# Attention values weighted token by token: probabilities stationary, nine value columns moving

## The reference

```python
qkv = layernorm(x) @ Wqkv                                  # q, k rotated
allowed = (dist <= 0) & (dist >= -63)                      # a window of 64 keys
weights = softmax(where(allowed, q @ k.T / sqrt(8), -inf))
x = x + (weights @ v) @ Wout
xf = layernorm(x)
routed = sum over 4 chosen experts of gate * (silu(xf @ wg) * (xf @ wu)) @ wd     # capacity 640 a expert
x = x + shared(xf) + routed
```

## Time and profile before

| what | before |
|---|---|
| median of 3 runs | 617.76 us (612.9 to 621.51) |
| profiled execution, its time | 617.19 us |
| its span | 615.1 us |
| PE busy | 515.4 us (84%) |
| PE weight loads busy | 423.6 us (69%) |
| DVE, ACT, POOL busy | 419.5, 323.7, 354.9 us |
| L939 matmuls, 2048 records | 41.5 us busy |
| L1010 transposes, 128 | 17.7 us busy |
| L667 copies, 32 | 18.7 us busy |
| mean granted clock of TensorE | 0.942 |

### The profile page before, as it was taken

How to read it: one execution, slowest core, us unless ns; L and a number is a source line. 1 busy time by engine, 2 the same in 40 slices (tenths; PEclk the granted TensorE clock), 3 DMA queues, 4 the chain that set the end, 5 groups by cost and what they waited for, 6 DMA issues and landing times.

```text
span 615.1 us, 20844 instructions
## 1 busy us (share of the span) xinstructions
PE 515.4 (84%) x7427; PEld 423.6 (69%) x7427; DVE 419.5 (68%) x1281; ACT 323.7 (53%) x832; POOL 354.9 (58%) x394
## 2 busy tenths in 40 slices
PE   3669888988788888887556889999999998999855
PEld 2446666656565666666424569999999998999544
DVE  5677579968888899968553566666666666565255
ACT  3336676756766776656534325454555544554300
POOL 7510114456666666667766704777777776777700
PEclk9959888988999999979977899999999998999988
DMA  7898998976776775530000023544345454442099
GB/s 249 244 243 231 243 244 235 275 202 196 221 202 201 206 219 148 139 85 24 21 10 9 10 86 112 167 125 131 118 141 163 153 163 138 140 116 89 14 349 334
DMA packets 79418, 98.33 MB, mean 160 GB/s; under 512 B 12098, under 2 KB 60000, under 8 KB 79217
## 3 DMA queue, kind: packets, MB, share of 16 engines
q1 hardware_dynamic: 65280, 82.92, 46.4%
q0 software_dynamic: 9216, 12.02, 6.3%
q10 hardware_dynamic: 4848, 2.40, 1.3%
HBM read 50.00 MB, written 54.30 MB: 170 GB/s over the span
## 4 chain that ended last, share of the span: by engine, by line
PE 51%; SPq 11%; POOL 10%; DMA 9%; issue 8%; DVE 5%; ACT 5%; POOLq 1%; DVEq 0%; ACTq 0%
PE banks L1122 18%; PE banks L1148 11%; SPq L352 5%; POOL expert_slots L491 4%; DMA rotated_keys<-parts 4%; DMA rload<-pair_results 3%; PE banks L1133 3%; POOL pout L544 3%; SPq L393 2%; PE banks L967 2%; PE banks L957 2%; PE banks L939 2%; SPq L344 2%; PE banks L862 2%; PE banks L849 2%
## 5 line engine op out<-in xcount | busy, mean ns | idle before, releaser
L625 POOL DMA_INDIRECT pair_results<-yout,yidx x160 | 158.5, 990 | 69.7 <-issue 40.9
L491 POOL DMA_INDIRECT expert_slots<-xfe,sidx x128 | 128.1, 1000 | 89.7 <-issue 43.6
L1122 PE MATMUL banks<-xgT_parts,wgu_parts 128*128 128x320 f32 x768 | 131.7, 320 | 2.2 <-DVE hact L1508 1.9
L1122 PEld LDWEIGHTS banks<-xgT_parts,wgu_parts 128*128 128x128 f32 x768 | 114.1, 190 | 5.0 <-DVE hact L1508 2.5
L1246 DVE TENSOR_REDUCE mx<-banks 128x8 f32<-128x1024 f32 x64 | 78.1, 1220 | 24.9 <-PE banks L889 24.9
L662 ACT ACTIVATE pt<-banks 128x512 f32<-128x512 f32 x128 | 69.4, 594 | 46.2 <-PE banks L920 45.6
L1508 DVE TENSOR_TENSOR hact<-hact,banks 128x320 f32<-128x320 f32 x128 | 56.6, 482 | 45.7 <-ACT hact L793 43.9
L812 ACT ACTIVATE yout<-banks,ypair 128x128 f32<-128x128 f32 x160 | 44.9, 372 | 76.1 <-PE banks L1148 76.1
L1148 PE MATMUL banks<-wdn,hact 128*128 128x128 f32 x640 | 76.6, 275 | 1.1 <-DVE hact L1508 1.1
L1148 PEld LDWEIGHTS banks<-wdn,hact 128*128 128x128 f32 x640 | 75.0, 192 | 1.3 <-issue 1.3
L793 ACT ACTIVATE hact<-banks 128x320 f32<-128x320 f32 x128 | 53.5, 452 | 30.6 <-PE banks L1122 28.8
(11 more groups left out here) (155 smaller groups left out, 960.3 us busy)
## 6 DMA issues: line engine op xcount, KB each, us to landing
expert_slots<-xg SPq DMA_DIRECT2D x32, 325.0 KB, 4.3
xg<-expert_slots SPq DMA_DIRECT2D x32, 325.0 KB, 2.9
pair_results<-zero SPq DMA_DIRECT2D x32, 256.0 KB
rload<-pair_results SPq DMA_DIRECT2D x16, 512.0 KB, 9.3
kS<-rotated_keys SPq DMA_DIRECT2D x32, 240.0 KB
qS<-rotated_queries SPq DMA_DIRECT2D x32, 192.0 KB
wgu<-in_L_ffn_wg_dram SPq DMA_DIRECT2D x32, 128.0 KB
wgu<-in_L_ffn_wu_dram SPq DMA_DIRECT2D x32, 128.0 KB
```

Source lines behind the costliest of these rows:

```text
L491: g.indirect_dma_start(out=slots_d, out_offset=bass.IndirectOffsetOnAxis(ap=sidx[:, m % NB, j, k:k + 1], axis=0), in_=xfe[:, m % NB, j, k, ...
L625: g.indirect_dma_start(out=pairs_d, out_offset=bass.IndirectOffsetOnAxis(ap=yidx[:, c, j:j + 1], axis=0), in_=yout[:, c, j, :], in_offset= ...
L1122: last = mm(bank[2 + 2 * w + h][:, 0:CH], wgu_parts[:, e.b, wp, w, h * P:(h + 1) * P], xgT_parts[:, e.b, xp, ch * CH:(ch + 1) * CH], start ...
```

## The change

The sides of the weighted sum are exchanged. Stationary are now 64 columns of probabilities (64 queries of a half), moving are nine columns: eight values and the ones. A result is 64 queries by 9, in bank 6 at 16 columns a head; the halves lie in partitions 0 to 63 and 64 to 127, so two column tiles are used in turn, and both tiles of a pair fit side by side in bank 6. Results have queries in rows, as `normalise` wants them. So `values_out` with its 2 copies a pair, the eight transposes a pair, the buffer `pvT` and the semaphores pv_evac and pvT_done go. `normalise` waits for the sums (pv_done). The wait for bank 7 (x1_ready), which stood at the transposes, stands before the Wout matmuls.

```diff
+    VW = PW // H
...
-        pvT = sb("pvT", [P, 2, 512])
...
-                def values_out(m, j):
-                    if m is not None:
-                        act.wait_ge(S.pv_done, 2 * m + (j + 1))
-                        wait(act, S.pvT_done, 2 * m - 1 + j)
-                        a.copy(pvT[:, j], bank[6][:, :]).then_inc(S.pv_evac, 1)
...
-                values_out(w, 1)
...
-                values_out(s, 0)
...
                     pe.wait_ge(S.exp_done, NU * m + 4 * j + NS * (c + 1))
-                    if c == 0:
-                        wait(pe, S.pv_evac, 2 * m + j)
+                    if j == 0 and c == 0:
                         wait(pe, S.onorm, m)
-                    for i in range(0, 4, 2):
-                        for hb in range(2):
-                            for ii in (i, i + 1):
-                                for st in range(NS):
-                                    h = NS * (4 * c + ii) + st
-                                    at = ii * P + hb * WIN
-                                    to = h // 4 * P + hb * WIN
-                                    last = mm(bank[6][32 * (h % 4):32 * (h % 4 + 1), to:to + WIN],
-                                              vals[:, m % 2, j, hb, h, :], pt[:, 4 * j + NS * c + st, at:at + WIN],
-                                              start=True, stop=True)
+                    for i in range(4):
+                        for st in range(NS):
+                            h = NS * (4 * c + i) + st
+                            for hb in range(2):
+                                at = i * P + hb * WIN
+                                to = j * PW + h * VW
+                                last = mm(bank[6][hb * WIN:(hb + 1) * WIN, to:to + DH + 1],
+                                          pt[:, 4 * j + NS * c + st, at:at + WIN], vals[:, m % 2, j, hb, h, 0:DH + 1],
+                                          start=True, stop=True)
...
-                if w is not None:
-
-                    pe.wait_ge(S.pv_evac, 2 * w + 2)
-                    pe.wait_ge(S.mT_evac, min(w + 2, NP))
-                    wait(pe, S.x1_ready, w)
-                    for j in range(2):
-                        for q in range(4):
-                            last = nc.tensor.transpose(bank[6 + j][:, q * P:(q + 1) * P], pvT[:, j, q * P:(q + 1) * P],
-                                                       ident)
-                        last.then_inc(S.pvT_done, 1)
...
                     pe.wait_ge(S.oT_evac, w + 1)
+                    wait(pe, S.x1_ready, w)
...
-                    sums = bank_pairs[3][:, :, :].rearrange("p j (h d) -> p j h d", h=H)
-                    dve.wait_ge(S.pvT_done, 2 * w + 2)
+                    sums = bank[6][:, :].rearrange("p (j h d) -> p j h d", j=2, h=H)
+                    dve.wait_ge(S.pv_done, 2 * w + 2)
```

More of the change, by code:

```diff
@@ L262, in block_kernel @@
         qk_written v_done v_evac v_prev vals_zero p1_scores p1_reduced negm mT_done mT_evac
-        p2_scores exp_done pv_done pv_evac pvT_done recip onorm oT_done oT_evac wout_done x1_ready ln2 powers_set w_pow off2_ready unit_ready xf_ready xf_copied
+        p2_scores exp_done pv_done recip onorm oT_done oT_evac wout_done x1_ready ln2 powers_set w_pow off2_ready unit_ready xf_ready xf_copied
         xfT_done xfT_evac router_done sc_ready route gate_exp gate_done marks_added sel_ready acc_ready pos_done
```

## The result

The changed kernel takes 628.24 us (median of four runs, 625.76 to 635.73); the kernel before took 616.47 us in the same series. The ratio is 1.020, with a 95% interval of 1.0145 to 1.0254: slower beyond the noise, but whether by the 2% that the prediction set stays open. A ratio leaves out executions more than 1.5% slower than the fastest of their kernel and a median does not, so the two need not agree. Predicted were 634 us, 622 to 644. The sign and the place were right, the size was 6 us too large.

What follows compares the result with a forecast made beforehand. Ten steps of a PE, ACT and POOL ring were taken to decide; 617.2 + 8.0 (slower sums) + 0.8 (sums at half clock) + 7.5 (clock falls) = 633.5, about 634 us, range 622 to 644.

Steps and rivals of the forecast that it cites:

- the ring: PE, ACT and POOL waiting on each other once per step of about 17 us, 126 to 294 us; ten steps decide.
- The sums on the ring: First tile's 64 weighted-sum records per step: 27.5 ns a record, 0.8 us more each, 8.0 us over ten steps.
- The removal worth nothing on the ring: Two ACT copies and eight PE transposes (1.09 us) per step are hidden, so removing them gains nothing in ten steps.
- The wait for the marks: PE's wait for POOL's marks of experts, 1.97 us before, was to grow to about 2.4 us.
- The mechanism of the clock: Longer waits for marks, without transposes ahead of them, make PE's granted clock fall oftener in the steps' first pieces.
- The price of the clock: Five more falls of PE's clock in the steps' first pieces at 1.5 us each: 7.5 us, bounds none to 10.5.
- The stalls: A 1.36 us PE stall behind one step's sums, which slower sums may fill; left to the range's lower end.
- that a step shortens: Sign against the forecast: any step shortening, or the clock staying at 1.00 in the first pieces named.
- Loads as said, clock no oftener: First rival: loads cost 8.8 us, clock falls no oftener than now; 626 us. Chance 0.29.
- The second: Rival: 64-column loads hide in the present 15.1 ns pace in all ten steps; about 617 us. Chance 0.07.
- the fourth: Rival: the loads of the two column tiles queue; 617.2 + 25 + 7.5, 650 us. Chance 0.06.
- The third, the turn on the ring: Rival: turning the values is on the ring, so ten steps lose 1.09 us each; 606 us. Chance 0.04.

Runs made afterwards that it cites:

- 3: Changed kernel with each half's 64 stationary columns cut into two of 32 on four column tiles, 128 records a tile: 641.74 us, ratio 1.0457.
- 6: Changed kernel with 32 moving columns a head instead of nine: 629.37 us; the same with tile 0's sums also issued behind the router: 607.86 us.
- 5: Changed kernel with tile 0's sums issued behind the router: 618.21 us; the same plus eight Wout transposes nobody reads: 629.71 us.
- 8: Kernel before with Wout matmuls behind second scores (1,0): 606.54 us; with tile 0's sums also behind the router and ACT's copy moved: 602.25 us.
- run 4: Kernel before, old sums, without copies and turn: 626.94 us, ratio 1.0176; the same with eight unread Wout transposes in the turn's place: 614.36 us, 0.9950.
- both pairs: Without and with eight unread PE transposes a pair: changed kernel 628.24 and 622.24 us; kernel before without copies and turn 626.94 and 614.36 us.
- run 2: Changed kernel with four plain f32 matmuls of 128 columns a pair, result unread, where the transposes stood: 621.49 us, ratio 1.0127.
- 1: Changed kernel with eight PE transposes a pair of a constant put back where they stood, result unread: 622.24 us, ratio 1.0148.
- two moves of order: Tile 0's sums behind the router and Wout matmuls behind second scores (1,0): old form 602.25 us; changed kernel with 32 moving columns 603.64 us.
- the moved kernel: Changed kernel with tile 0's sums issued behind the router, ahead of second scores (1,1): 618.21 us, ratio 0.9995.

## Why the prediction was right, and where it wasn't

- **The sums on the ring: right.** 29 ns a record ((2040 - 203) / 63) against 27.5 predicted; 0.88 us more a step against 0.8. Nine steps at 0.88 and one at half clock with 1.66 make 9.6 us against 8.8. Runs 3 and 6 point to the loads: another moving width doesn't change the pace, and loads of half the width, on twice the tiles, bring it to 8.5 ns. That the price is paid because of the place shows in 5 and 8: off the ring the old form and the new one with wide moving sides take the same time.
- **The removal worth nothing on the ring: right, but not the whole of it.** Copies and turn were hidden, as run 4 shows from the other side: with idle work in place of the turn, and no copies, the kernel stands at 0.995 of before, not surely faster. The wait for the marks grew to 2.3 us as predicted (2.4).
- **The mechanism of the clock: right in kind.** That taking work out ahead of the marks lowers the clock is shown by both pairs: 0.90 to 0.97 with the new sums, 0.86 to 0.95 with the old ones. It is no chance of one execution: over the whole span, the runs that the ratios count show 0.909 to 0.912 without the idle transposes and 0.923 to 0.944 with them, and with the old sums 0.899 to 0.909 and 0.930 to 0.941.
- **The price of the clock: the term that was mis-sized.** The sentence "The four steps at 162.1, 179.7, 197.0 and 246.1 then look like those that fell; for the thinner work elsewhere I take a fifth" failed. Two more of the ten first pieces had a fall, those beginning at 165.4 and 288.2, not five, so it was five pieces of ten in place of the seven to nine named as a sign. The guess rested on the length of the wait, and that alone does not decide: 2.31 us of waiting stood ahead of a fall once and ahead of none twice. The falls that came lasted longer, though: the piece at 145.70 took 7.10 us where such a piece took 6.10 before. Read from the steps, the clock cost 1.4 us at 165.4 and 1.0 at 145.7. Two more are whole steps less their sums' growth: (17.02 - 14.78) - 0.88 = 1.4 us at 288.2 and (19.23 - 16.76) - 1.66 = 0.8 us at 269.0. Together 4.6 us, against 7.5.
- **The stalls: left to the range, and they did fill.** 2.17 us on the chain, the 1.36 among them, are gone. One of the prediction's own signs of being wrong came with it, that a step shortens: the one with the 0.81 us stall took 17.01 us in place of 17.29. What filled the stalls was not tried alone; that PE's sequencer gets ahead during slower sums is a reading, no more.
- **The sum as it was.** 9.6 + 4.6 - 2.2 = 12.0 us, where the ten steps measured 10.84; the 1.2 us over have no place in this account, and it is luck that the medians lie 11.8 apart. On record stood 8.8 + 7.5 = 16.3. The difference of 4.3 is 2.9 of clock and 2.2 of stalls, less 0.8 of sums.
- **The rivals.** "Loads as said, clock no oftener" (626) came nearer in time, 2 us off against the forecast's 6, but not in what it said: the clock did fall more, 0.90 for 0.96, and with the clock kept up the kernel takes 621.5 to 622.2 us. The rule on transposes that stood behind it is what run 2 takes away. The second and the fourth fell by the 1.97 us. The third, the turn on the ring, fell by run 4 and by the undisturbed steps, which went from 16.2 us up to 17.0 and not down by 1.09.

What stays open is what the chip goes by. Waits ahead of the marks matter (1, 4), and so does the width of what streams when there is no wait (5 against 6), while the width alone did nothing where the waits were long (6). No run gives a rule that names the steps beforehand.

## What to carry to other kernels

Before taking work off an engine that waits anyway, ask what that work does besides its result: PE's turn of the values cost nothing on the path, and without it the ten steps grew by 11.7 us through the clock. Exchanging the sides of a matmul trades moved columns for loaded ones, so price it by the loads and by the number of column tiles, at the place on the ring where it stands. If it is the place that makes it dear, move it first: two moves of order brought the old form, and the new one with wide moving sides, to 602 to 604 us, 1.1% and 1.8% under the kernel before by the ratios, the first of them not quite clear of the noise.

## What was not expected of the hardware

- The clock fell with PE never idle. In the moved kernel PE worked through the 6 us ahead of 173.9 and through the 10.20 us at half clock behind it, and the one difference in code to the kernel whose clock stood at 1.00 there was nine moving columns in place of 32.
- With weight loads of 64 f32 columns on two column tiles a record comes every 29 ns, whether nine or 32 columns move; with loads of 32 columns on four tiles every 8.5 ns with nine moving and every 15.1 with 64.
- Twice as many records for the same sums took 19 us off their busy time (72.0 to 52.9) and put 14.0 us of unexplained idle time in front of them alone; the kernel became 2.5% slower by the two ratios.
